# Feed-forward to attention: the first group's loads ahead of the last chunk's turn, its row products between the last query operations

## The chip, the core and the metric

The kernel runs on one core of one Trainium2 chip, as one program. The metric is the time of one execution on the device in microseconds. A core has engines that run their own instruction streams and meet only at semaphores: TensorE (PE, matrix products into the eight PSUM banks), VectorE (DVE), ScalarE (ACT), GpSimd (POOL), and the sync engine SP, which in this kernel issues every DMA, one instruction after another.

## What is computed

Four steps over x, 4 sequences of 512 tokens of 512 channels, each added to x behind a gate tanh(g):

```python
x = x + jnp.tanh(g_xattn[0]) * _L0_xattn_ref(4, 512, 512, L0_xattn_w, L0_xattn_u, _layernorm(x), ctx_2048)
x = x + jnp.tanh(g_ffn[0]) * _L0_ffn_ref(_layernorm(x), L0_ffn_w1, L0_ffn_w2, L0_ffn_w3)
x = x + jnp.tanh(g_xattn[1]) * _L1_xattn_ref(_layernorm(x), ctx_2048, wq, bq, wkv, bkv, wp, bp)
x = x + jnp.tanh(g_ffn[1]) * _L1_ffn_ref(_layernorm(x), gamma, W)
```

The change lies between the second and the third. The second is a feed-forward of 2048 hidden channels with activations rounded to 8 bits in groups of 64: silu(q(x) W1) * q(x) W2, rounded again, times W3. The third is attention with 16 heads of 32 channels:

```python
q = _qdq(x) @ _qdq(wq).T + bq            # _qdq: 8-bit rounding of each token's row
kv = cond @ wkv.T + bkv                  # keys and values, from the context
attn = softmax(einsum('bnhd,bmhd->bhnm', q, k) * scale)
o = einsum('bnhm,bmhd->bnhd', attn, v)
out = _qdq(o) @ _qdq(wp).T + bp
```

## The kernel before

**Tiles.** The 2048 tokens are 16 token tiles of 128 (TOK), four (TB) to each of 4 sequences (BATCH). The 512 channels are four blocks of 128 (DB), and each block holds one group of four heads (HG), so attention runs over 4 x 4 = 16 groups (b, g). The hidden channels are four chunks of 512 (FC). Numbers in brackets below are (token tile, chunk) or (sequence, group).

**Feed-forward.** For each token tile i and chunk j, TensorE multiplies by W1 and W2 (`up`, L1028 to L1040, line of the products L1038), ScalarE and VectorE apply silu, product and rounding, ScalarE and GpSimd write the result as a high and a low half (`high` L749, `lo_part` L532), SP turns it with a transposing DMA (`turn_h`, L389 to L394), and TensorE multiplies by W3 (`down`, L1042 to L1049) into bank 5 for even and bank 6 for odd token tiles, which VectorE adds to X (`residual`, L1475). `down(i, j)` waits for the turn `hT_in[j]`. The order of work on each engine is the order in which the program writes it; semaphores only make an engine wait.

**Queries, interleaved with it.** For token tile u: `q_stats` (DVE, L1483), `q_rstd` (POOL, L539), `q_norm` (ACT, L754), `q_max` (DVE, L1490), `q_diag` (POOL, L546), `q_round` (ACT, L760), `q_ints` (DVE, L1498), `q_turn` (PE, L1051, transposes L1056 and a diagonal product L1058), `q_operands` (ACT, L764), `q_project` (PE, L1060), `q_full` (DVE, L1503), `q_bias` (ACT, L771), `q_low` (POOL, L551). Each feeds the next. They follow the feed-forward by two to four token tiles, so the last of them stand in a tail written out by hand on every engine, behind the loop: L1086 to L1096 on TensorE, L1550 to L1564 on VectorE, L818 to L829 on ScalarE, L585 to L593 on GpSimd.

**Attention.** For a group (b, g) SP brings keys (`load_kv`, three DMAs L411 and one of values L414) and queries (`load_q`, twelve DMAs L423) into KS and QS, 16 in all. KS and QS lie in the memory of W1 and W2, so the first loads wait until the last `up` is done (`b_ps`, L404). For stability of the softmax the kernel first finds the maximum of each query's scores: 16 row products for a group (`rows`, L1101, products L1108, into banks 0, 1 and 5 in turn; each waits until the maximum of the third last has been read), and VectorE reduces each (`maxima`, L1568, L1574). TensorE turns the 16 columns of maxima (`c_turn`, L1111, L1116), ScalarE and VectorE write them as a high and a low half (`c_out` L835, `c_low` L1577), and SP sends them as two more rows of QS (`send_c`, L427, DMAs L432). GpSimd has set the matching rows 96 and 97 of KS to 1 (L597). Only then can the 16 score products of the group run (`scores`, L1119, L1125; the first waits for `c_in`), with the maxima already inside, followed by exponentials on ScalarE (L866), the products with V (`weigh`, L1135) and the sums (L1144, L1154, additions on GpSimd L610). Each group is 16 slots; the row products of the next groups are dealt out over the slots (`ROWS`, L300, with a lead of `LEAD` = 6 rows), so that the first row product of group g + 2 stands in slot 8 of group g, and `c_turn` of group g + 1 behind slot 9.

**Order on SP at the boundary.** All hidden turns up to `turn_h(15, 3)`; the wait for `b_ps`; loads of groups 0, 1, 2, 3 of sequence 0; `send_c(0, 0)` (L434 to L437); then `feed` (L439), whose first act is `send_c(0, 1)`.

**Order on TensorE at the boundary.** `down(15, 3)`, the last query operations, a wait for `area_free` (the last read of ffs by the tail of VectorE; L1099), waits that the banks are free (L1202 to L1204), 16 + 6 row products, the wait for the ones, `c_turn(0, 0)`, and the groups.

Of the kernel before, what the change touches and what calls it, by code (L numbers as in the profile page):

```python
# [8 lines left out]
ALU = mybir.AluOpType  # L9
# [7 lines left out]
DB = D // P  # L17
# [14 lines left out]
def up_to(eng, sem, value):  # L32

    if isinstance(value, int) and value <= 0:
        return
    eng.wait_ge(sem, value)


class Chain:
# [5 lines left out]
    def link(self, ins):  # L45

        ins.then_inc(self.sem, 1)
        self.n += 1
        self.eng.wait_ge(self.sem, self.base + self.n)
# [11 lines left out]
def flamingo_kernel(nc, x, ctx_2048, g_xattn, g_ffn, w, u, w1, w2, w3, wq, bq, wkv, bkv, wp, bp, gamma, wl, out):  # L61
    stack = ExitStack()
    with stack:
# [255 lines left out]
        def _(sp):  # L319
# [62 lines left out]
            def turn_x(i, a):  # L382

                sp.wait_ge(xhi, i + 1)
                sp.wait_ge(xlo, i + 1)
                up_to(sp, b_ps, FC * (i - 1))
                sp.dma_start_transpose(XQT[a], PHL.rearrange("p h d -> p (h d)")).then_inc(xT_in[a], 16)

            def turn_h(i, j):  # L389

                sp.wait_ge(hi_done, FC * i + j + 1)
                sp.wait_ge(lo_done, FC * i + j + 1)
                up_to(sp, down_ps, FC * i + j - 3)
                sp.dma_start_transpose(HT[j], HLb[j].rearrange("p h d -> p (h d)")).then_inc(hT_in[j], 16)  # L394

            sp.wait_ge(ff_scales, 1)
            turn_x(0, 0)
            for i in range(TOK):
                for j in range(FC):
                    turn_h(i, j)  # L400
                    if j == 0 and i < TOK - 1:
                        turn_x(i + 1, (i + 1) % 2)

            sp.wait_ge(b_ps, FC * TOK)  # L404

            def load_kv(b, g, first):

                if not first:
# [18 lines left out]
            def send_c(b, g):  # L427

                sp.wait_ge(ct_ready, b * DB + g + 1)
                sp.wait_ge(ct_low, b * DB + g + 1)  # L430
                for h in range(2):
                    sp.dma_start(QS[96 + h:97 + h, HG * g:HG * g + HG, :], CT[h][0:HG, :]).then_inc(c_in, 16)  # L432

            for g in range(DB):  # L434
                load_kv(0, g, True)
                load_q(0, g)
            send_c(0, 0)  # L437

            def feed(b, first, last):  # L439
                for g in range(DB):  # L440
# [19 lines left out]
        def _(pool):  # L460
# [85 lines left out]
            def q_diag(u):  # L546
                pool.wait_ge(qs3, u + 1)
                up_to(pool, sx_ps, u)
                nc.gpsimd.tensor_tensor(DIAG, id32[:, :], QSC[:, 0:1].to_broadcast([P, P]), ALU.mult).then_inc(diag3, 1)

            def q_low(u):  # L551
                pool.wait_ge(q_hi, u + 1)
                nc.gpsimd.tensor_tensor(held[:, 0:1], held[:, 1:2], held[:, 1:2], ALU.add)
                cols = bass.ds(u * P, P)
                nc.gpsimd.tensor_tensor(QALL[:, 1, :, cols], QB, QALL[:, 0, :, cols], ALU.subtract).then_inc(q_lo, 1)
# [5 lines left out]
            def tiles(k, last):  # L561
                for a in range(2):
                    i = 2 * k + a
                    for j in range(FC):
                        if j == 0 and there(i - 3):
                            q_diag(i - 3)
                        if j == 1 and not (last and a == 1):
                            x_turned(pool, k, a)
                            prep_lo(i + 1)
                        if j == 1 and not last:  # L570
                            prep(i + 2)
                        if j == 2 and there(i - 2):
                            q_rstd(i - 2)
                        if j == 2 and there(i - 4):
                            q_low(i - 4)
                        lo_part(i, j)
# [5 lines left out]
                tiles(k, False)  # L582
            step.turns_over(TOK // 2 - 3)
            tiles(TOK // 2 - 1, True)
            q_diag(TOK - 3)  # L585
            q_rstd(TOK - 2)
            q_low(TOK - 4)
            q_diag(TOK - 2)
            q_rstd(TOK - 1)
            q_low(TOK - 3)  # L590
            q_diag(TOK - 1)
            q_low(TOK - 2)
            q_low(TOK - 1)  # L593


            pool.wait_ge(q_lo, TOK)
            nc.gpsimd.memset(KS[96:98, :, :], 1.0).then_inc(ks_ones, 1)  # L597
            pool.wait_ge(ks_ones, 1)

            def add_weights(b, first, last):  # L600
                for g in range(DB):
# [33 lines left out]
        def _(act):  # L635
# [124 lines left out]
            def q_round(u):  # L760
                act.wait_ge(qs3, u + 1)
                nc.scalar.activation(LX, LX, ACT.Copy, bias=RND, scale=QR[:, 0:1]).then_inc(rnd3, 1)
# [58 lines left out]
            q_operands(TOK - 3)  # L821
            q_round(TOK - 2)
            q_norm(TOK - 1)
            q_bias(TOK - 3)
            q_operands(TOK - 2)
            q_round(TOK - 1)
            q_bias(TOK - 2)
            q_operands(TOK - 1)
            q_bias(TOK - 1)  # L829


# [94 lines left out]
        def _(pe):  # L926
# [156 lines left out]
            with pe.Fori(2, TOK // 2 - 1) as k:  # L1083
                tiles(k, False, False)
            tiles(TOK // 2 - 1, False, True)
            q_project(TOK - 4)  # L1086
            down(TOK - 1, 0, 1)
            down(TOK - 1, 1, 1)
            q_turn(TOK - 3)
            down(TOK - 1, 2, 1)  # L1090
            down(TOK - 1, 3, 1)
            q_project(TOK - 3)
            q_turn(TOK - 2)
            q_project(TOK - 2)
            q_turn(TOK - 1)
            q_project(TOK - 1)  # L1096


            pe.wait_ge(area_free, 1)  # L1099

            def rows(b, g, n):  # L1101

                j, t, r = n // TB, n % TB, (b * DB + g) * 16 + n
# [15 lines left out]
            def scores(b, g, t, j):  # L1119

                n = b * DB + g
                if t == 0 and j == 0:
                    pe.wait_ge(c_in, n * 32 + 32)
                up_to(pe, exp_done, n * 16 + HG * t + j - 1)
                mm(bank[2 + j % 2][:, :], KS[0:98, HG * g + j, t * P:t * P + P], QS[0:98, HG * g + j, :],  # L1125
                   start=True, stop=True).then_inc(st_ps, 1)
# [51 lines left out]
            def attend(b, first, last):  # L1178
                for g in range(DB):
                    opening, closing = first and g == 0, last and g == DB - 1  # L1180
                    ahead = coming(b, g)
                    for slot in range(16):
# [16 lines left out]
                        if slot == 9 and not closing:  # L1199
                            c_turn(*following(b, g))  # L1200

            pe.wait_ge(down_read, TOK)  # L1202
            pe.wait_ge(h_done, FC * TOK)
            pe.wait_ge(qf_ready, TOK)  # L1204
            for n in range(16):
                rows(0, 0, n)
            for n in range(LEAD):
                rows(0, 1, n)
            pe.wait_ge(ks_ones, 1)
            c_turn(0, 0)  # L1210
            for b in range(BATCH):
                attend(b, b == 0, b == BATCH - 1)
            weigh(BATCH - 1, DB - 1, TB - 1)
# [45 lines left out]
        def _(dve):  # L1259
# [292 lines left out]
            q_ints(TOK - 3)  # L1552
            q_full(TOK - 4)
            q_max(TOK - 2)
            residual(TOK - 1, 1)
            q_stats(TOK - 1)
            q_full(TOK - 3)
            q_ints(TOK - 2)
            link(ts(LSC, LSC, 1.0 / 127.0, None, ALU.mult))
            ts(LSC, LSC, TG[:, 3:4], None, ALU.mult).then_inc(area_free, 1)  # L1560
            q_max(TOK - 1)
            q_full(TOK - 2)
            q_ints(TOK - 1)
            q_full(TOK - 1)  # L1564

            flat = lambda a: a.rearrange("p a d -> p (a d)")

            def maxima(b, g, n):  # L1568
# [46 lines left out]
                        i = (b - 1) * TB + g  # L1615
                        reduce(OM[:, bass.ds(i, 1)], OALL[:, bass.ds(i, 1), :], AX.X, ALU.max, apply_absolute_value=True)

            for n in range(16):
                maxima(0, 0, n)
            for n in range(LEAD):  # L1620
                maxima(0, 1, n)
            c_low(0, 0)
            for b in range(BATCH):
                attend(b, b == 0, b == BATCH - 1)
            def scales(n, m):
# [106 lines left out]
```

## Time and profile before

| | |
|---|---|
| Median of 3 runs | 993.82 us (992.88 to 997.99) |
| Profiled execution | 988.19 us, its span 986.4 us |
| Mean granted TensorE clock in it | 0.931 of full speed |
| Busy in the span: PE, DVE, ACT, POOL | 83%, 78%, 59%, 49% |
| Feed-forward, last hidden turn issued | about 576 us into the span |
| First score product of attention | about 618 us into the span |

The profile's page gives for each engine its busy time, the costliest lines with their mean duration, and the chain of work that ended last: from the last instruction back, at each step to what released it. The timeline lists an engine's instructions in order of time as start, duration, engine, line, operation, operands and count; in brackets stands how long the engine was idle before it and what released it. An entry with a count merges neighbours, so its duration over its count is a pace. SPq is SP issuing DMAs: the duration is that of the issue, not of the transfer. The windows give busy time per engine in a stretch and the granted clock of TensorE, where 1.00 is 2.4 GHz and 0.50 is 1.2 GHz.

### The profile page before, as it was taken

To read this page: it belongs to the slowest core of one execution; us is meant where nothing else is said; L and a number is where in the kernel's file an instruction comes from. 1 tells how busy PE (TensorE), PEld (TensorE's weight loads), DVE (VectorE), ACT (ScalarE), POOL (GpSimd) and SP (SyncE) were. 2 spreads that over 40 slices of the span, in tenths; PEclk is the share of its full clock that TensorE was granted. 3 is DMA by queue.
4 is the path that set the end of the run, shared out by engine and by line. 5 is a ranking of instruction groups with operands and counts; after the bars stand their busy time and mean duration, and the time that the engine had idled before them with its cause. 6 is when DMAs were issued, how large, how long until landed. Compare 5 with 4: busy or idle time off the path is not lost.

```text
span 986.4 us, 15339 instructions
## 1 busy us (share of the span) xinstructions
PE 816.1 (83%) x4423; PEld 356.8 (36%) x4423; DVE 766.1 (78%) x1499; ACT 579.3 (59%) x1025; POOL 483.7 (49%) x556
## 2 busy tenths in 40 slices
PE   1279989818999999999999966899999999865654
PEld 1245445403444444454444431222222222222221
DVE  3969999866899989999999756677777777635885
ACT  2368988733445556565666452566666666656662
POOL 1186564212344444343443333575757575746561
PEclk9589999969999999999999985899999999997886
DMA  8548996622233332323233233112121211000111
GB/s 281 210 118 213 236 215 184 185 66 45 57 62 71 58 64 53 64 53 64 53 61 67 54 95 97 37 52 77 54 77 54 75 55 44 2 1 0 47 59 64
DMA packets 165162, 84.49 MB, mean 86 GB/s; under 512 B 116961, under 2 KB 149873, under 8 KB 165105
## 3 DMA queue, kind: packets, MB, share of 16 engines
q1 hardware_dynamic: 165104, 83.81, 33.7%
q8 instruction: 26, 0.43, 0.2%
q14 instruction: 32, 0.25, 0.1%
HBM read 37.50 MB, written 12.58 MB: 51 GB/s over the span
## 4 chain that ended last, share of the span: by engine, by line
PE 54%; DVE 9%; issue 4%; SPq 4%; ACT 4%; DMA 3%; POOL 1%; DVEq 0%; ACTq 0%; POOLq 0%
PE bank L1038 21%; PE bank L1047 10%; PE bank L1135 5%; PE bank L1108 5%; PE bank L1125 4%; SPq L423 3%; DMA A<-B 3%; PE bank L1144 2%; PE bank L1154 2%; PE bank L1065 1%; DVE X L1683 1%; SPq L432 1%; DVE B L1582 1%; DVE B L1668 1%; ACT B L839 1%
## 5 line engine op out<-in xcount | busy, mean ns | idle before, releaser
L1038 PE MATMUL bank<-A,B 128*128 128x512 f16 x1024 | 232.9, 381 | 18.6 <-DMA B<-B 14.8
L1574 DVE TENSOR_REDUCE B<-bank 128x1 f32<-128x512 f32 x256 | 167.6, 683 | 68.6 <-PE bank L1108 68.5
L866 ACT ACTIVATE A<-bank 128x512 f32<-128x512 f32 x256 | 143.8, 593 | 101.9 <-PE bank L1125 97.1
L537 POOL TENSOR_TENSOR B<-B 128x512 f16<-128x512 f32 x64 | 75.5, 1180 | 207.0 <-ACT B L752 153.0
L1038 PEld LDWEIGHTS bank<-A,B 128*128 128x128 f16 x1024 | 100.2, 98 | 141.5 <-issue 18.3
L610 POOL TENSOR_TENSOR B<-A 128x512 f32<-128x512 f32 x64 | 79.4, 1271 | 94.8 <-ACT A L866 94.8
L1047 PE MATMUL bank<-A,B 128*128 128x512 f16 x512 | 120.6, 379 | 0.0
L1125 PE MATMUL bank<-A 98*128 98x512 f16 x256 | 93.3, 385 | 25.4 <-DMA A<-B 13.8
L747 ACT ACTIVATE bank<-B 128x512 f32<-128x512 f32 x64 | 38.5, 602 | 124.2 <-DVE B L1467 123.9
L1108 PE MATMUL bank<-A 96*128 96x512 f16 x256 | 98.8, 408 | 1.2 <-DVE B L1506 1.1
L610 POOL TENSOR_TENSOR B<-B,A 128x512 f32<-128x512 f32 x64 | 79.1, 1267 | 0.0
L1047 PEld LDWEIGHTS bank<-A,B 128*128 128x128 f16 x512 | 49.5, 98 | 54.2 <-DMA B<-B 0.3
L1135 PE MATMUL bank<-A,B 128*32 128x512 f32 x512 | 68.2, 605 | 1.0 <-ACT A L866 1.0
L1462 DVE SCALAR_TENSOR_TENSOR bank<-bank,ffs,B 128x512 f32<-128x512 f32 x64 | 48.3, 755 | 14.6 <-PE bank L1038 11.4
L1473 DVE SCALAR_TENSOR_TENSOR B<-bank,B 128x512 f32<-128x512 f32 x64 | 44.2, 691 | 17.1 <-ACT bank L747 15.7
L1016 PE MATMUL bank<-B 128*128 128x512 f16 x192 | 44.2, 380 | 12.4 <-DVE B L1368 12.4
L1108 PEld LDWEIGHTS bank<-A 96*128 96x128 f16 x256 | 23.0, 99 | 79.8 <-DVE B L1574 69.7
L1125 PEld LDWEIGHTS bank<-A 98*128 98x128 f16 x256 | 24.8, 98 | 72.0 <-ACT A L866 37.6
L499 POOL TENSOR_SCALAR B<-X,mv,rs 128x128 f32<-128x128 f32 x64 | 49.9, 795 | 1.2 <-DVE WLT L1296 1.2
L742 ACT ACTIVATE B<-bank,ffs 128x512 f32<-128x512 f32 x64 | 43.0, 671 | 9.5 <-PE bank L1038 9.3
L752 ACT CAST B<-B 128x512 f16<-128x512 f32 x64 | 39.5, 618 | 11.3 <-DVE B L1473 10.9
L1464 DVE TENSOR_REDUCE B<-bank 128x8 f32<-128x512 f32 x64 | 44.3, 691 | 2.2
(232 smaller groups left out, 1495.3 us busy)
## 6 DMA issues: line engine op xcount, KB each, us to landing
B<-in_L_ffn_w_dram SPq DMA_DIRECT2D x48, 256.0 KB, 3.2
A<-k_parts SPq DMA_DIRECT2D x48, 128.0 KB, 2.5
A<-B SPq DMA_DIRECT2D x192, 32.0 KB, 1.9
X<-in_x_dram SPq DMA_DIRECT2D x4, 1024.0 KB, 13.6
B<-in_ctx_dram SPq DMA_DIRECT2D x16, 256.0 KB, 5.2
k_parts<-B SPq DMA_DIRECT2D x16, 256.0 KB, 4.6
v_rows<-B SPq DMA_DIRECT2D x16, 256.0 KB, 3.0
B<-v_rows SPq DMA_DIRECT2D x16, 256.0 KB, 3.2
```

The source lines that it names most:

```text
L499: last_ = nc.gpsimd.tensor_scalar(XN[:, t, cols], X[:, i, cols], mv[:, i:i + 1, 0], rs[:, i:i + 1], ALU.subtract, ALU.mult)
L537: nc.gpsimd.tensor_tensor(HLb[j][:, 1, :], Db[j % 2], HLb[j][:, 0, :], ALU.subtract).then_inc(lo_done, 1)
L610: nc.gpsimd.tensor_tensor(ACC[j], PR[j] if t == 1 else ACC[j], PR[(HG * t + j) % 8], ALU.add).then_inc(acc_done, 1)
L866: nc.scalar.activation(PR[(HG * t + j) % 8], bank[2 + j % 2][:, :], ACT.Exp, scale=SCALE).then_inc(exp_done, 1)
L1038: last = mm(bank[2 * n + q][:, :], XQT[a][:, m, :], wt[:, m % DB, j * 512:j * 512 + 512], start=(m == 0), stop=(m == 2 * DB - 1))
L1047: last = mm(bank[5 + q][:, :], HT[j][:, m, :], W3T[:, DB * j + m % DB, :], start=(j == 0 and m == 0), stop=(j == FC - 1 and m == 2 * DB - 1))
L1108: mm(bank[ROW_BANKS[r % 3]][:, :], QS[0:96, HG * g + j, t * P:t * P + P], KS[0:96, HG * g + j, :], start=True, stop=True).then_inc(row_ps, 1)
L1125: mm(bank[2 + j % 2][:, :], KS[0:98, HG * g + j, t * P:t * P + P], QS[0:98, HG * g + j, :], start=True, stop=True).then_inc(st_ps, 1)
L1135: last_ = mm(bank[6][DH * j:DH * j + DH, :], VB[:, t, (HG * g + j) * DH:(HG * g + j + 1) * DH], PR[(HG * t + j) % 8], start=(t == 0), stop ...
L1462: stt(H, H, C2, SAb[q], ALU.mult, ALU.mult).then_inc(h_done, 1)
L1464: link(reduce(gsm[:, 0, :], grouped(H), AX.X, ALU.max, apply_absolute_value=True))
L1574: reduce(NMX[g % 2][:, t, j:j + 1], bank[ROW_BANKS[r % 3]][:, :], AX.X, ALU.max, negate=True).then_inc(row_max, 1)
```

## The change

On SP the loads of group 0 stand before the last hidden turn, behind the wait for `b_ps`; the loads of group 1 behind that turn; then `send_c(0, 0)`; then the loads of groups 2 and 3. On TensorE and VectorE the 16 row products and maxima of group (0, 0) are dealt out in the tail: two ahead of `down(15, 3)` and `residual(15)`, six between the last query operations, eight behind the last projection. TensorE no longer waits for `area_free`, but waits for the banks that the rows take (`d_done`, `down_read` of tile 14) ahead of the first. `c_turn(0, 0)` stands ahead of the six row products of group (0, 1), and on VectorE `c_low(0, 0)` behind the first of their maxima. On ScalarE `q_bias(13)` and `q_bias(14)` stand one place later, on VectorE `q_ints(14)` stands ahead of `q_full(13)`. On GpSimd the one memset of the ones becomes four, one for each group of heads, put between the last `q_low`; TensorE's wait for them moves into `scores`.

```diff
@@ SP @@
+            sp.wait_ge(ff_scales, 1)
+            turn_x(0, 0)
+            for i in range(TOK):
+                for j in range(FC):
+                    if i == TOK - 1 and j == FC - 1:
+                        sp.wait_ge(b_ps, FC * TOK)
+                        load_kv(0, 0, True)
+                        load_q(0, 0)
+                    turn_h(i, j)
+                    if j == 0 and i < TOK - 1:
+                        turn_x(i + 1, (i + 1) % 2)
+            load_kv(0, 1, True)
+            load_q(0, 1)
+            send_c(0, 0)
+            for g in range(2, DB):
                 load_kv(0, g, True)
                 load_q(0, g)
-            send_c(0, 0)
@@ GpSimd @@
+            def ones_under(g):
+
+                pool.wait_ge(b_ps, FC * TOK)
+                pool.wait_ge(diag3, TOK)
+                if g > 0:
+                    pool.wait_ge(q_lo, TOK - DB + 1 + g)
+                nc.gpsimd.memset(KS[96:98, HG * g:HG * g + HG, :], 1.0).then_inc(ks_ones, 1)
+                pool.wait_ge(ks_ones, g + 1)
...
-            q_low(TOK - 3)
             q_diag(TOK - 1)
-            q_low(TOK - 2)
-            q_low(TOK - 1)
-
-
-            pool.wait_ge(q_lo, TOK)
-            nc.gpsimd.memset(KS[96:98, :, :], 1.0).then_inc(ks_ones, 1)
-            pool.wait_ge(ks_ones, 1)
+            ones_under(0)
+            for u in (TOK - 3, TOK - 2, TOK - 1):
+                q_low(u)
+                ones_under(u - TOK + 4)
@@ ScalarE @@
             q_norm(TOK - 1)
-            q_bias(TOK - 3)
             q_operands(TOK - 2)
             q_round(TOK - 1)
+            q_bias(TOK - 3)
+            q_operands(TOK - 1)
             q_bias(TOK - 2)
-            q_operands(TOK - 1)
             q_bias(TOK - 1)
@@ TensorE: the tail of before is taken out, and scores has @@
                     pe.wait_ge(c_in, n * 32 + 32)
+                    if b == 0:
+                        pe.wait_ge(ks_ones, g + 1)
@@ TensorE @@
+            q_project(TOK - 4)
+            down(TOK - 1, 0, 1)
+            down(TOK - 1, 1, 1)
+            q_turn(TOK - 3)
+            down(TOK - 1, 2, 1)
+            pe.wait_ge(d_done, FC * TOK)
+            pe.wait_ge(down_read, TOK - 1)
+            first_rows(0, 2)
+            down(TOK - 1, 3, 1)
+            q_project(TOK - 3)
+            first_rows(2, 3)
+            q_turn(TOK - 2)
+            first_rows(3, 4)
+            q_project(TOK - 2)
+            first_rows(4, 6)
+            q_turn(TOK - 1)
+            first_rows(6, 8)
+            q_project(TOK - 1)
+            first_rows(8, 16)
             pe.wait_ge(down_read, TOK)
             pe.wait_ge(h_done, FC * TOK)
             pe.wait_ge(qf_ready, TOK)
-            for n in range(16):
-                rows(0, 0, n)
+            c_turn(0, 0)
             for n in range(LEAD):
                 rows(0, 1, n)
-            pe.wait_ge(ks_ones, 1)
-            c_turn(0, 0)
@@ VectorE @@
+            first_maxima(0, 2)
+            residual(TOK - 1, 1)
+            q_stats(TOK - 1)
+            q_ints(TOK - 2)
+            q_full(TOK - 3)
+            link(ts(LSC, LSC, 1.0 / 127.0, None, ALU.mult))
+            ts(LSC, LSC, TG[:, 3:4], None, ALU.mult).then_inc(area_free, 1)
+            first_maxima(2, 3)
+            q_max(TOK - 1)
+            first_maxima(3, 4)
+            q_full(TOK - 2)
+            q_ints(TOK - 1)
+            first_maxima(4, 8)
+            q_full(TOK - 1)
+            first_maxima(8, 16)
+            maxima(0, 1, 0)
+            c_low(0, 0)
+            for n in range(1, LEAD):
                 maxima(0, 1, n)
-            c_low(0, 0)
```

## Rows read from the trace of the kernel before

**Rows 1.** The page, section 4: the chain that ended last, by line.

```profile
PE bank L1038 21%; PE bank L1047 10%; PE bank L1135 5%; PE bank L1108 5%; PE bank L1125 4%; SPq L423 3%; DMA A<-B 3%; PE bank L1144 2%; PE bank L1154 2%; PE bank L1065 1%; DVE X L1683 1%; SPq L432 1%; DVE B L1582 1%; DVE B L1668 1%; ACT B L839 1%
```

**Rows 2.** The same chain in order of time, 560 to 640 us: start, us, what.

```profile
615.80 0.69 SPq L432
...
618.29 0.61 PE bank L1125
```

**Rows 3.** Timeline of SP, two windows: start, us, engine, line, operation, count.

```profile
569.96 6.48 SPq L394 DMA_TRANSPOSE B<-B  x2
...
575.21 1.23 SPq L394 DMA_TRANSPOSE B<-B  x1
...
576.49 1.53 SPq L411 DMA_DIRECT2D A<-k_parts  x3
...
586.95 1.53 SPq L411 DMA_DIRECT2D A<-k_parts  x3
...
606.14 1.53 SPq L411 DMA_DIRECT2D A<-k_parts  x3
```

**Rows 4.** DMA issues of the whole kernel: operands, count, KB each, us to landing.

```profile
A<-B SPq DMA_DIRECT2D x192, 32.0 KB, 1.9
...
B<-B SPq DMA_TRANSPOSE x80, 3.1
```

**Rows 5.** Timeline of TensorE, 576 to 626 us, in the columns of rows 3.

```profile
576.68 3.62 PE L1047 MATMUL bank<-A,B 128*128 128x512 f16 x16
580.45 1.07 PE L1065 MATMUL bank<-B,WQT 128*128 128x128 f16 x16 [0.15 <-ACT B L769]
...
591.11 0.74 PE L1058 MATMUL bank<-B,ones 128*128 128x128 f32 x2
593.36 1.89 PE L1065 MATMUL bank<-B,WQT 128*128 128x128 f16 x16 [1.51 <-ACT B L769]
596.33 12.74 PE L1108 MATMUL bank<-A 96*128 96x512 f16 x22 [1.09 <-DVE B L1506]
608.87 1.06 PE L1116 MATMUL bank<-id,B 128*4 128x128 f32 x4
...
625.12 0.38 PE L1108 MATMUL bank<-A 96*128 96x512 f16 x1
```

**Rows 6.** Timeline of VectorE, 580 to 612 us.

```profile
580.78 0.73 DVE L1481 SCALAR_TENSOR_TENSOR X<-bank,ffs,X 128x512 f32<-128x512 f32 x1
...
584.84 0.69 DVE L1494 TENSOR_REDUCE B<-B 128x1 f32<-128x512 f32 x1 [1.14 <-ACT B L758]
...
595.28 0.69 DVE L1506 TENSOR_TENSOR B<-bank,B 128x512 f32<-128x512 f32 x1 [4.63 <-PE bank L1065]
596.96 13.25 DVE L1574 TENSOR_REDUCE B<-bank 128x1 f32<-128x512 f32 x22 [0.99 <-PE bank L1108]
610.91 0.68 DVE L1582 TENSOR_TENSOR B<-bank,B 4x512 f16<-4x512 f32 x1 [0.71 <-ACT B L839]
```

**Rows 7.** Windows, attention's groups 0 and 1: stretch, us, busy by engine, clock, DMA.

```profile
618.29:632.83 14.54, 13.41 (x61) 3.86 (x62) 10.58 (x17) 9.00 (x17) 9.34 (x8) 0.87 0.01 2
632.83:649.26 16.43, 15.37 (x93) 4.63 (x94) 11.90 (x20) 10.29 (x20) 11.55 (x10) 1.00 0.23 64
```

**Rows 8.** Windows of 2 us: where the granted clock fell and came back.

```profile
584.00:586.00 2.00, 0.12 (x2) 0.00 (x0) 1.00 (x3) 2.00 (x5) 0.00 (x0) 0.62 0.18 49
...
608.00:610.00 2.00, 2.00 (x7) 0.69 (x6) 2.00 (x4) 0.00 (x0) 0.00 (x0) 0.50 0.80 236
...
622.00:624.00 2.00, 1.96 (x13) 0.45 (x11) 1.98 (x4) 1.68 (x3) 0.51 (x1) 1.00 0.00 0
```

**Rows 9.** Timeline of ScalarE, 592 to 600 us.

```profile
592.55 0.58 ACT L768 COPY B<-bank 128x512 f16<-128x512 f16 x1
...
598.32 1.28 ACT L832 ACT_TABLE_LOAD   x1
```

**Rows 10.** Timeline of GpSimd, the memset of the ones.

```profile
599.73 6.92 POOL L597 MEMSET A<- 2x8192 f16 x1
```

More of the change, by code:

```diff
@@ L394, in turn_h @@
                 sp.dma_start_transpose(HT[j], HLb[j].rearrange("p h d -> p (h d)")).then_inc(hT_in[j], 16)
[L396 to L404, printed above, removed]
             def load_kv(b, g, first):
@@ L432, in send_c @@
                     sp.dma_start(QS[96 + h:97 + h, HG * g:HG * g + HG, :], CT[h][0:HG, :]).then_inc(c_in, 16)
-            for g in range(DB):
+            sp.wait_ge(ff_scales, 1)
[13 more added lines that the diff above has]
+            for g in range(2, DB):
                 load_kv(0, g, True)
                 load_q(0, g)
-            send_c(0, 0)
             def feed(b, first, last):
@@ L1085, in _ @@
             tiles(TOK // 2 - 1, False, True)
[L1086 to L1099, printed above, removed]
             def rows(b, g, n):
@@ L1200, in attend, with first_rows @@
                             c_turn(*following(b, g))
+            def first_rows(n, m):
+                for r in range(n, m):
+                    rows(0, 0, r)
+            q_project(TOK - 4)
[17 more added lines that the diff above has]
+            first_rows(8, 16)
             pe.wait_ge(down_read, TOK)
@@ L1554, in _ @@
             q_max(TOK - 2)
[L1555 to L1564, printed above, removed]
             flat = lambda a: a.rearrange("p a d -> p (a d)")
@@ L1616, in attend, with first_maxima @@
                         reduce(OM[:, bass.ds(i, 1)], OALL[:, bass.ds(i, 1), :], AX.X, ALU.max, apply_absolute_value=True)
-            for n in range(16):
-                maxima(0, 0, n)
-            for n in range(LEAD):
+            def first_maxima(n, m):
+                for r in range(n, m):
+                    maxima(0, 0, r)
+            first_maxima(0, 2)
[16 more added lines that the diff above has]
+            for n in range(1, LEAD):
                 maxima(0, 1, n)
-            c_low(0, 0)
             for b in range(BATCH):
```

## The prediction

> **What bounds the kernel now.** I read the chain that ended last first. TensorE leads it over the whole span, but one line of the sync queue, L423, holds 3% of it, about 29 us [rows 1]. The same chain in order of time shows where it ends: the sync engine (SP) issues the small transfer of L432 at 615.80, and the first score product (L1125) starts at 618.29 [rows 2]; the 36 us ahead of 615.80 are the issuing of loads. So at this boundary the issuing of DMAs is the bound, not any engine that computes. The timeline of SP gives the pieces: the turn of the last hidden chunk, turn_h(15,3), is issued at 575.21, then four groups of 16 loads each. The second, third and fourth start 9.6 us apart (586.95, 596.55, 606.14), the first took 10.5, and send_c(0,0) is issued behind the fourth at 615.80 [rows 2, 3]. Next the computing engines: TensorE's query operations end at 595.3, its 22 row products run from 596.33 to 609, paced by VectorE's maxima (22 in 13.25 us, 0.60 each), and the row of maxima is ready to send at 611.6, 4.2 us before SP is free [rows 5, 6]. Hence the loads delay the first score by only 4.2 us; without them the chain of the maxima would be next.
>
> **What has to be costed is the second send, not the first.** In both versions send_c(0,1) stands on SP behind the loads of groups 2 and 3. Before, these were long past: group 0 of attention took 14.54 us, and group 1's first score ran at 632.83. From there a group takes 16.43 us [rows 7]. After the change the loads of groups 2 and 3 (2 x 9.6 us) stand between send_c(0,0) and send_c(0,1). If send_c(0,0) is issued at T, then the second send is issued at T + 1.36 (two issues and their gaps) + 19.2 = T + 20.6, and group 1's first score starts 2.5 us behind its issue, as 615.80 and 618.29 stood, at T + 23.1 [rows 2, 3]. What follows is the same work at the same 16.43 us, so the change is worth 632.83 - (T + 23.1): break-even is **T = 609.7**.
>
> **T, step by step.**
> Load of group 0: SP issues turn_h(15,2) from 569.96 for 1.23 us; the weights' last use is past by 569.1, so the load starts at 571.2 and ends at 580.8 (9.6; with the first group's 10.5 it would be 581.7). Its last issue lands 1.9 us after it starts, at 582.1 [rows 3, 4].
> Turn of the last chunk: issued at 575.21 before, 580.9 now. It lands about 3.1 us behind its issue [rows 4], at 584.0. What is queued behind it is down(15,3), 5.7 us later than before. Two row products stand ahead of it on TensorE and wait for the load, 578.4 to 582.1, but they are done before 584.0 and cost nothing of their own.
> Clock: the granted clock fell to its lower level (1.2 GHz) at about 584.5, 3 us after the dense work ended at 581.5; here dense work ends at 578.4 and 3.7 idle us follow. I take the lower level, 0.50 in the rows [rows 5, 8]. Then down(15,3), 8 products, takes 3.4 us instead of 1.7 (sixteen took 3.62 at the upper level; a projection took 1.07 there and 1.89 at the lower [rows 5]) and ends at 587.4.
> Query chain of token tile 15: its residual starts at 587.5. From residual to q_max took 4.06 us (580.78 to 584.84) through statistics, GpSimd and ScalarE, unchanged by the new order, so q_max(15) starts at 591.6 [rows 6]. ScalarE's q_norm(15) is done then, q_operands(14) follows (0.8, from 592.55 to TensorE's 593.36 [rows 5, 9]), TensorE's q_project(14) runs 592.4 to 594.3, and q_full(14) and q_ints(15), 0.7 and 0.4, end at 595.4. q_turn(15) takes 1.1 (591.11 + 0.74, begun at 590.7) to 596.6, q_operands(15) goes to 597.5, q_project(15) and q_full(15) take 1.92 + 0.69 as before: 600.1 [rows 5, 6]. Before, q_full(15) ended at 595.97, so the query chain ends **4.1 us later**, although it started 5.7 to 6.7 later: ScalarE's reordering takes q_bias(13) out from between.
> Maxima: eight of sixteen are dealt into gaps of this chain, eight are left: 8 x 0.60 = 4.8, to 604.9, where 13.25 stood before. The dealt ones lie in waits of VectorE (4.6 us stood before q_full(15) alone [rows 6]).
> Maxima row: c_turn's start to the end of c_low took 2.7 us (608.87 to 611.59 [rows 5, 6]); now one maximum stands between, hidden by ScalarE's copy except 0.2. So **T = 608**.
> The other edits: q_bias(15) follows q_full(15) and q_low(14) and ends on ScalarE at about 603.5, with the 1.28 us table load [rows 9] 604.8, ahead of the copy at 606.5. The memset (6.92 us for all heads [rows 10]) becomes four; I take a quarter each, 1.7 us, with 0 to 1 us more per piece as bounds, since no smaller one is in the trace; group 0's is over by 596 and GpSimd's q_low is off the path until 604.9. The new SP wait on send_c(0,0) blocks the loads of groups 2 and 3 while SP is idle from 591.8 to 608: this is the price of the change, and it is in the 23.1.
>
> **The sum.** Group 1's first score at 608 + 23.1 = 631.1: 1.7 us earlier. On the way TensorE waits twice. Slot 8 of group 0 needs group 2's load, T + 12.3, and would be reached at T + 2.5 + 6.8 (618.29 to 625.12 before [rows 2, 5]): 3.0 us idle. And at group 1's first score it waits from about T + 19.2 to T + 23.1: 3.9 us. The clock fell after such a gap at 584.5, and in attention it came back at 622, 3.7 us behind the first score [rows 2, 8]; 3.7 us at half rate cost 1.9, if every product is on the path. Some are not: TensorE has about 1 idle us per group (15.37 busy of 16.43 [rows 7]). I take 1.2, bounds 0 and 2.4. Net gain 0.5 us: the profiled run's 988.2 becomes 987.7. The median of the shown runs is 993.8, 5.6 above; on that scale **993.3**.
>
> The page "DMA: Bandwidth & Descriptors" of the Trainium skill (Queues, rings and completion order) says that a transfer's completion is written only after all earlier writes of that DMA engine. This speaks against putting 16 loads ahead of the turn. The loads' 1.9 us to landing, against the turn's 3.1, would put them down first, so by the rule and by the rows the turn lands at 584.0 alike; were the loads slower to drain, T would grow by that.
>
> **Rivals.**
> *Clock stays up, short chain (0.12).* If TensorE's five dense microseconds after 584 bring the clock back, or it never falls, down(15,3) takes 1.7, each projection 1.07, and ScalarE's queue becomes the limit: q_project(15) ends at 595.9 and T is 604.1. Group 1 starts at 627.2, 5.6 us earlier: 988.2, or about 990 with the clock lost in the waits. For it: dense work was followed by the upper level at 622. Against: 12.7 us of row products paced by VectorE were not [rows 5, 8]. Most of this case is a gain of 2 to 5 us, within 0.5%.
> *The held-back chunk costs more than is won (0.20).* Mechanism: turn_h(15,3) and all of tile 15's query chain behind the load. It decides from T = 609.7, that is with 1.7 us more than I sum: 0.9 if the first load again takes 10.5, and any microsecond that rows between the query operations take from ScalarE's or VectorE's waits. With T = 610.6 and both waits costing the clock (2.4), group 1's work is 3.3 us late: 997.1.
> *SP's second and third loads do not bind (0.05).* If the whole 7.7 us by which the first score comes earlier (T + 2.5 = 610.5 against 618.29) reached the end: 986.1. Against it stands only the order on SP, 38 issues with none faster than 0.43 us, and I see no way round it.
> *The change does nothing at all (in the forecast).* SP's order makes the end of the boundary T + 23.1, and T moves by less than 2 us: that is close to what I forecast.
>
> **How the numbers follow.** Forecast 0.63 for a net of -1.4 to +2.6 us; rivals 0.12, 0.20, 0.05. A measurement of this kernel tells 0.5%, 5 us, from no change. Faster by more: the third rival and a third of the first, 0.09. Slower by more needs T above 612: 0.05. Range: 987.5 (short chain, 988.2) to 998.0 (the slow rival, 997.1), each rounded outwards because the runs shown lay 992.9 to 998.0.
>
> **What would show it.** Right: SP's last turn near 581, a gap on SP before send_c(0,0) at about 608, two waits of TensorE on loads at slot 8 and on L432 in front of group 1, group 1's first score near 631, 16.4 us per group after. Wrong: send_c(0,0) before 604 or after 611; granted clock at the upper level from 588 to 605; group 1's first score more than 3 us from 631; or a group of attention that is no longer 16.4 us.

## The result: 0.3% slower

The changed kernel takes 997.8 us (median of 19 runs, 995.5 to 1000.7), the kernel before 994.9 in 19 runs of the same sessions (991.8 to 998.3). The ratio is **1.0031, 95% interval 1.002 to 1.0043**: about 3 us more. The time lies in the stated range, but the sign was forecast the other way (0.5 us less).

| | before | after |
|---|---|---|
| Median of 19 runs | 994.91 us | 997.82 us |
| Span of the profiled execution | 986.4 us | 994.8 us |
| Mean granted clock | 0.931 | 0.934 |

The two spans are 8.4 us apart, which is more than the change costs. To see only what the change touches, I measure a **boundary** inside each trace: from the start of q_ints(13) on VectorE (t0; the last work on VectorE that is the same in both) to the first score product of group (0,2), from where each group takes 16.43 us again. Before, that is 575.70 to 649.26 us: 73.56. After, 580.67 to 657.97: 77.30, so **3.74 us more**. The 5.0 us by which t0 itself differs belong to unchanged work; in the nine traces below t0 lies between 575.55 and 583.18.

The kernel before, t0 and the first score product of groups 1 and 2:

```profile
575.70 0.41 DVE L1501 TENSOR_SCALAR B<-B 128x512 f16<-128x512 f32 x1
...
632.83 0.38 PE L1125 MATMUL bank<-A 98*128 98x512 f16 x1 [0.41 <-ACT A L866]
...
649.26 0.38 PE L1125 MATMUL bank<-A 98*128 98x512 f16 x1 [0.41 <-DMA A<-B]
```

The changed kernel, t0:

```profile
580.67 0.41 DVE L1516 TENSOR_SCALAR B<-B 128x512 f16<-128x512 f32 x1
```

A boundary is read from one profiled execution, a ratio from all runs of a version. For every version below the two give the same sign, and sizes within 2 us of each other, so tenths of a microsecond in a boundary are exact readings of one trace and not averages.

The timeline of SP in the changed kernel, in the columns of rows 3 (L394 the turns, L401 keys, L413 queries, L422 the row of maxima):

```profile
574.92 1.23 SPq L394 DMA_TRANSPOSE B<-B  x1
576.21 1.53 SPq L401 DMA_DIRECT2D A<-k_parts  x3
...
586.07 1.28 SPq L394 DMA_TRANSPOSE B<-B  x1
587.39 1.54 SPq L401 DMA_DIRECT2D A<-k_parts  x3
...
615.54 1.35 SPq L422 DMA_DIRECT2D A<-B  x2
616.93 1.38 SPq L401 DMA_DIRECT2D A<-k_parts  x3
...
628.48 8.29 SPq L413 DMA_DIRECT2D A<-B  x12
636.87 1.32 SPq L422 DMA_DIRECT2D A<-B  x2
```

send_c(0,0) goes out 34.87 us behind t0 instead of 40.10 [rows 2]: 5.2 us earlier. Then the two groups of loads fill SP from 616.93 to 636.8, and only behind them send_c(0,1) is issued, 21.3 us after the first. TensorE in the same stretch (L1120 scores, L1101 row products):

```profile
618.04 0.61 PE L1120 MATMUL bank<-A 98*128 98x512 f16 x1
...
627.77 0.38 PE L1101 MATMUL bank<-A 96*128 96x512 f16 x1 [2.04 <-issue]
...
639.37 0.61 PE L1120 MATMUL bank<-A 98*128 98x512 f16 x1 [4.55 <-DMA A<-B]
...
657.97 0.38 PE L1120 MATMUL bank<-A 98*128 98x512 f16 x1 [0.41 <-DMA A<-B]
```

The first score runs 37.4 us behind t0, where it had run at 42.6. TensorE then stands 2.0 us at slot 8 (marked as issue; the last query load of group 2 was issued at 625.80 and lands about 1.9 us later) and 4.55 us in front of group 1, and group 1's first score comes at 58.7 where it came at 57.1. All 5.2 us of the earlier send are gone, and 1.6 more. The rest of the loss lies in group 1, and it is the clock; windows as in rows 7 and 8:

```profile
637.00:638.00 1.00, 0.00 (x0) 0.00 (x0) 0.00 (x0) 0.00 (x0) 0.00 (x0) 0.64 0.13 35
...
643.00:644.00 1.00, 1.00 (x3) 0.15 (x1) 0.72 (x2) 0.00 (x0) 0.00 (x0) 0.50 0.16 27
644.00:645.00 1.00, 1.00 (x9) 0.17 (x8) 0.56 (x1) 0.60 (x1) 0.00 (x0) 0.95 0.96 279
...
639.37:657.97 18.60, 17.54 (x92) 4.85 (x93) 11.57 (x19) 10.06 (x19) 9.79 (x8) 0.87 0.21 57
657.97:674.40 16.43, 15.37 (x92) 4.61 (x92) 11.90 (x20) 10.30 (x20) 11.10 (x10) 1.00 0.23 66
```

In the wait the granted clock fell to 1.2 GHz and was back at 2.4 GHz only at 644; group 1 took 18.60 us instead of the 16.43 of rows 7, with the same products. All of it lies in the first products: from the group's first score to its first sum (L1149; L1154 in the kernel before) it took 4.65 us where it had taken 2.49, and eight products with V took 1.93 us instead of 1.06. Together 1.57 + 2.17 = 3.74 us.

### The profile page after: what moved, and what is told of

The parts are those of the page before. It is cut to its first block, busy times and chain, and to the rows that moved or that the text cites. A ratio compares the mean times of both kernels' runs of the same rounds, so it can differ in the third digit from the quotient of the medians.

```text
span 994.8 us, 15350 instructions
## 1 busy us (share of the span) xinstructions
PE 821.2 (83%) x4423; PEld 359.6 (36%) x4423; DVE 767.2 (77%) x1499; ACT 579.9 (58%) x1025; POOL 485.2 (49%) x559
## 4 chain that ended last, share of the span: by engine, by line
PE 53%; DVE 9%; issue 5%; SPq 4%; ACT 4%; DMA 3%; POOL 1%; DVEq 0%; ACTq 0%; POOLq 0%
PE bank L1046 21%; PE bank L1055 10%; PE bank L1130 5%; PE bank L1101 4%; PE bank L1120 4%; DMA A<-B 2%; SPq L413 2%; PE bank L1139 2%; PE bank L1149 2%; PE bank L1073 1%; SPq L422 1%; DVE X L1705 1%; DVE B L1586 1%; DVE B L1690 1%; PE bank L1109 1%
## 5 line engine op out<-in xcount | busy, mean ns | idle before, releaser
L1046 PE MATMUL bank<-A,B 128*128 128x512 f16 x1024 | 233.0, 381 | 18.6 <-DMA B<-B 14.8
L1120 PE MATMUL bank<-A 98*128 98x512 f16 x256 | 94.5, 390 | 21.4 <-ACT A L874 10.9
L1101 PE MATMUL bank<-A 96*128 96x512 f16 x256 | 97.1, 405 | 8.1 <-DMA A<-B 3.8
L1101 PEld LDWEIGHTS bank<-A 96*128 96x128 f16 x256 | 23.1, 100 | 83.2 <-DVE B L1578 66.1
L1120 PEld LDWEIGHTS bank<-A 98*128 98x128 f16 x256 | 25.0, 99 | 67.3 <-ACT A L874 36.5
```

What stands on the lines that cost most here:

```text
L1046: last = mm(bank[2 * n + q][:, :], XQT[a][:, m, :], wt[:, m % DB, j * 512:j * 512 + 512], start=(m == 0), stop=(m == 2 * DB - 1))
L1101: mm(bank[ROW_BANKS[r % 3]][:, :], QS[0:96, HG * g + j, t * P:t * P + P], KS[0:96, HG * g + j, :], start=True, stop=True).then_inc(row_ps, 1)
```

## The experiments

Two theories. **A**: the two loads between the sends on SP cost the time; everything hangs on T, the issue of send_c(0,0), and on what stands behind it. **B**: the held-back turn and the dealt-out rows cost it, whatever the order of the loads. Each run's numbers are counted from its own t0. "S1" is the first score of group 1.

| kernel | send_c(0,0) | send_c(0,1) | S1 | boundary | ratio to before |
|---|---|---|---|---|---|
| before | 40.10 | 54.60 | 57.13 | 73.56 | 1 |
| changed | 34.87 | 56.20 | 58.70 | 77.30 | 1.0031 [1.002, 1.0043] |
| a_load2_first | 34.92 | 50.36 | 52.88 | 69.32 | 0.9953 [0.994, 0.9966] |
| b_send_early | 35.96 | 57.16 | 59.66 | 77.69 | 1.0047 [1.0032, 1.0063] |
| b_load3_late | 35.98 | 50.96 | 53.49 | 69.92 | 0.9953 [0.9939, 0.9966] |
| a_second_qf | 32.32 | 53.71 | 56.21 | 74.86 | 1.0019 [1.0008, 1.0031] |
| b_hold_load3_late | 43.19 | 58.10 | 60.63 | 77.06 | 1.0026 [1.0013, 1.0038] |
| b_cturn_first | 33.80 | 49.36 | 51.88 | 68.31 | 0.9928 [0.9903, 0.9953] |
| v_turn_first | 29.13 | 43.99 | 46.51 | 62.94 | 0.989 [0.9874, 0.9906] |

**1. The changed kernel, only one group of loads behind the send.**

```diff
-            load_kv(0, 1, True)
-            load_q(0, 1)
-            send_c(0, 0)
-            for g in range(2, DB):
+            for g in range(1, DB - 1):
                 load_kv(0, g, True)
                 load_q(0, g)
+            send_c(0, 0)
+            load_kv(0, DB - 1, True)
+            load_q(0, DB - 1)
```

> The changed kernel, with the loads of group 2 put ahead of send_c(0,0), and only those of group 3 behind it. I measure the boundary from the start of q_ints(13) on VectorE (the same work before it in all kernels) to the first score product of group 2: 73.56 us before the change, 77.30 after. Theory A, sends behind loads: send_c(0,1) stood behind two loads, now behind one, which is done before the second row of maxima is ready. send_c(0,0) stays at 34.9 us, group 1's first score comes 17.0 us behind it (2.5 to the first score, 14.5 for group 0) instead of 23.8, with no wait of TensorE for a load at slot 8 and no fall of the clock: boundary 68.3 us, 5.2 below before and 9.0 below the change, ratio to before 0.995. Theory B, the held-back last turn and the dealt-out rows cost the time: the order of these loads changes nothing, boundary 77, ratio 1.003.

Measured: the first send where it was (34.92), the second 5.8 us earlier, boundary 69.32, ratio 0.9953. Sixteen DMA instructions, moved ahead of the two of one send, turn a loss of 0.3% into a gain of 0.5%. Its TensorE has no wait at slot 8, and in front of group 1's first score one of 0.41 us, as the kernel before had:

```profile
629.09 0.39 PE L1120 MATMUL bank<-A 98*128 98x512 f16 x1 [0.32 <-ACT A L874]
...
632.79 0.38 PE L1120 MATMUL bank<-A 98*128 98x512 f16 x1 [0.41 <-DMA A<-B]
```

Theory B would have left the boundary at 77. The miss of 1.0 us against my 68.3 lies between the first score and S1, 15.5 us instead of 14.5. The granted clock came back only between 623 and 624 there (0.76 in that window), about 6 us behind the first score at 617.33, where it had been 3.7 before.

**2. The kernel before, with nothing but the early send.**

```diff
-            for g in range(DB):
+            for g in range(2):
                 load_kv(0, g, True)
                 load_q(0, g)
             send_c(0, 0)
+            for g in range(2, DB):
+                load_kv(0, g, True)
+                load_q(0, g)
```

> The kernel before, with nothing of the change but the place of send_c(0,0): behind the loads of groups 0 and 1, ahead of those of groups 2 and 3. Theory A: the row of maxima is ready 35.9 us into the boundary and is sent then, 4.2 earlier than before, but send_c(0,1) stands behind two loads: group 1's first score 23.8 us behind it at 59.7, before 57.13, and with the clock lost in the wait (2.2, as in the changed kernel) a boundary of 78.4 us, 4.8 above before; ratio 1.005. Theory B: nothing of the query chain is touched, the send is earlier, so the boundary is 4 us shorter, 69.4, ratio 0.996.

Measured: 77.69 and 1.0047, against 78.4 and 1.005 expected. No query operation is touched, no turn held, no row dealt out; the early send alone makes the kernel slower, by sending the first row 4.1 us earlier. TensorE shows the same two waits:

```profile
627.87 0.38 PE L1111 MATMUL bank<-A 96*128 96x512 f16 x1 [2.44 <-issue]
...
639.34 0.39 PE L1128 MATMUL bank<-A 98*128 98x512 f16 x1 [4.43 <-DMA A<-B]
...
657.37 0.38 PE L1128 MATMUL bank<-A 98*128 98x512 f16 x1 [0.41 <-DMA A<-B]
```

From 639.34 to 657.37 is 18.03 us for group 1, again over 16.43. The windows have the clock at 1.00 through the wait and at 0.50 from 640 to 643: here it fell only when the products had begun again. That is a second measurement of what such a wait costs through the clock, 1.6 us.

**3. The kernel before, one group of loads behind the send.** As run 2, with `range(3)` and `range(3, DB)`.

> The kernel before, with only the loads of group 3 moved behind send_c(0,0). Theory A: send_c(0,0) when its row is ready, at 35.9 us of the boundary; group 3's loads are over 11 us later, before the second row is ready at about 14.4; group 1's first score 17.0 us behind the send; boundary 69.4 us, 4.2 below before, ratio 0.996. Theory B gives the same for this one; a boundary of 73.6 would say that the loads in front of the send were not what the first score waited for.

Measured: 69.92, ratio 0.9953.

```profile
618.15 1.34 SPq L432 DMA_DIRECT2D A<-B  x2
...
633.13 1.32 SPq L432 DMA_DIRECT2D A<-B  x2
```

Moving one group of loads is a gain, moving two is a loss. And this simplest edit, one group of loads moved on one engine, has the same ratio as run 1, which carries all of the change's reordering: holding, dealing out, moving c_turn and the new order on ScalarE together bring the first send from 35.98 to 34.92, 1.06 us.

**4. What made T later than I summed.** The changed kernel with a second buffer for the scaled query of tile 14. q_full(14) then waits for no q_bias, and q_full(15) for q_bias(13) and no longer for q_bias(14). (q_bias is changed to read QF2 for tile 14; not shown.)

```diff
+        QF2 = part(D, F32, "p (k t) -> p k t", k=DB)
+        fourteen = lambda u: isinstance(u, int) and u == TOK - 2
...
             def q_full(u):
                 dve.wait_ge(qp_ps, u + 1)
-                up_to(dve, q_hi, u)
-                tt(QF, bank[7][:, :].rearrange("p (k t) -> p k t", k=DB),
+                if not fourteen(u):
+                    up_to(dve, q_hi, u - 1 if isinstance(u, int) and u == TOK - 1 else u)
+                tt(QF2 if fourteen(u) else QF, bank[7][:, :].rearrange("p (k t) -> p k t", k=DB),
```

> The changed kernel with a second buffer for the scaled query of token tile 14, so that q_full(14) no longer waits for q_bias(13), which the change had put behind q_norm(15) and q_round(15) on ScalarE. Theory A2, this wait is the largest part of what the send of the first row came later than I summed: q_full(14) starts when q_project(14) is done and VectorE is free, 2.4 us earlier than in the changed kernel; send_c(0,0) 2.3 us earlier (32.6 us into the boundary against 34.9), and as everything hangs on this send, the boundary 75.0 against 77.30; ratio to before 1.001. Rival: ScalarE's queue or the slower q_ints is next at once, and send_c(0,0) moves by less than 1 us.

Measured: send_c(0,0) at 32.32, 2.55 us earlier, boundary 74.86. The changed kernel around the wait that is gone here: TensorE's q_project(14) (L1073), the last step of q_bias(13) on ScalarE (L787), and VectorE (L1521 q_full, L1516 q_ints):

```profile
597.73 1.07 PE L1073 MATMUL bank<-B,WQT 128*128 128x128 f16 x16 [1.81 <-ACT B L777]
...
600.47 0.62 ACT L787 CAST B<-B 128x512 f16<-128x512 f32 x1
...
601.19 0.69 DVE L1521 TENSOR_TENSOR B<-bank,B 128x512 f32<-128x512 f32 x1 [2.46 <-ACT B L787]
601.80 1.01 DVE L1516 TENSOR_SCALAR B<-B 128x512 f16<-128x512 f32 x1
```

and with the second buffer:

```profile
602.10 0.69 DVE L1524 TENSOR_TENSOR B<-bank,B 128x512 f32<-128x512 f32 x1 [0.93 <-PE bank L1075]
602.70 0.56 DVE L1518 TENSOR_SCALAR B<-B 128x512 f16<-128x512 f32 x1
```

q_full(14) starts 18.92 us behind t0 instead of 20.52, released by the projection and not by ScalarE. Of the 2.55 us, 1.60 are this wait. Another 0.46 come from q_ints(15), which took 0.56 us and not 1.01, and the remaining 0.49 lie in front of q_full(15), which in the changed kernel was released by q_bias(14) on ScalarE and here by its projection. Run 1 shows from the other side that the projection did not bind in the changed kernel: its q_project(14) took 1.89 us, 0.8 more, and q_full(14) started at 20.58 all the same. Everything behind moved with the send, as theory A has it.

**5. The price of the held-back turn alone.** Run 3, and the 16 loads of group 0 ahead of `turn_h(15, 3)` as in the change. The diff is against run 3 and shows only the held turn.

```diff
                 for j in range(FC):
+                    if i == TOK - 1 and j == FC - 1:
+                        sp.wait_ge(b_ps, FC * TOK)
+                        load_kv(0, 0, True)
+                        load_q(0, 0)
                     turn_h(i, j)
```

> The kernel before with only the loads of group 3 behind send_c(0,0), as in the run with that change alone (boundary 69.92 us, send at 35.98), and now also the 16 loads of group 0 ahead of the last hidden turn. It costs what the hold costs by itself, without dealt-out rows to pay for it. My sum: the turn 5.9 us later, down(15,3) at the lower clock, residual(15) at 12.3 us of the boundary instead of 5.1, the query chain behind it 7.2 to 7.7 later, send_c(0,0) at 43.6 us, boundary 77.6, ratio to before 1.004. The rival, that the hold is cheap because other query work fills the wait: send_c(0,0) by 38 us, boundary 72, ratio 0.998.

Measured: residual(15) at 12.28 us instead of 5.08, send_c(0,0) 7.21 us later than in run 3, boundary 77.06 (7.1 more). In the timeline of VectorE the whole tail has slid, with the wait for down(15,3) in front and the 22 maxima behind as in rows 6:

```profile
593.64 0.75 DVE L1486 SCALAR_TENSOR_TENSOR X<-bank,ffs,X 128x512 f32<-128x512 f32 x1 [7.12 <-PE bank L1052]
...
609.84 13.24 DVE L1579 TENSOR_REDUCE B<-bank 128x1 f32<-128x512 f32 x22 [0.98 <-PE bank L1113]
```

So the hold is not cheap: it costs 7.2 us of the chain, and what run 1 adds to it, dealt-out rows, the earlier c_turn and the new order on ScalarE, returns 8.3 (43.19 to 34.92). Theory B is right about the price and wrong about the verdict: the price is paid back, and 1.1 us more.

**6. The earlier c_turn alone.** Run 3, and c_turn(0,0) ahead of the six rows of group (0,1) on TensorE, c_low(0,0) behind the first of their maxima on VectorE. The diff shows TensorE's part against run 3.

```diff
+            c_turn(0, 0)
             for n in range(LEAD):
                 rows(0, 1, n)
             pe.wait_ge(ks_ones, 1)
-            c_turn(0, 0)
```

> The kernel before with the loads of group 3 behind send_c(0,0), and c_turn(0,0) and c_low(0,0) put ahead of the row products and maxima of group (0,1), as the change does. With the send no longer waiting for loads, the chain of the maxima sets it: six maxima of 0.60 us less in front, one of them kept ahead of c_low at a cost of 0.2: send_c(0,0) at 32.5 us of the boundary instead of 35.98, boundary 66.4 against 69.92, ratio to before 0.993. The rival, that the first scores then wait for those six rows anyway: boundary above 69.

Measured: 33.80, boundary 68.31, ratio 0.9928. Of the 3.5 us that I expected 2.2 came. c_turn now has to wait for the last maximum, where before six rows had stood between, and starts 2.2 us earlier instead of 3.6:

```profile
611.73 1.01 PE L1119 MATMUL bank<-id,B 128*4 128x128 f32 x4 [1.18 <-DVE B L1577]
```

Without holding or dealing anything its boundary is 1.0 us shorter than that of run 1, and its first send 1.1 us earlier. The two ratios point the same way, but their intervals overlap. By the traces, then, holding, dealing out and the new order on ScalarE together are a small loss in run 1. They need not be: run 4 takes 2.55 us off the same chain by removing the waits for q_bias. Run 1 with the second buffer was not measured.

**7. A version that beats both.** Keys and values of group 0 ahead of the turn, its query loads behind; loads of group 2 ahead of the send; rows dealt out where VectorE waits in the trace of before; ScalarE's order as before; the memsets behind the last q_low. TensorE has four rows behind q_turn(14), two behind q_project(14), three behind q_turn(15) and seven behind q_project(15).

```diff
                     if i == TOK - 1 and j == FC - 1:
                         sp.wait_ge(b_ps, FC * TOK)
                         load_kv(0, 0, True)
-                        load_q(0, 0)
                     turn_h(i, j)
...
+            load_q(0, 0)
@@ VectorE @@
             q_max(TOK - 1)
+            first_maxima(0, 4)
             q_full(TOK - 2)
             q_ints(TOK - 1)
+            first_maxima(4, 9)
             q_full(TOK - 1)
+            first_maxima(9, 16)
```

> The changed kernel with four repairs: the last hidden turn goes out before the query loads of group 0 (only its three key loads and one value load stand ahead of the turn, in 4 us in which SP waits anyway); the loads of group 2 ahead of send_c(0,0); the rows of group (0,0) dealt out where VectorE waits in the trace of before (four between q_max(15) and q_full(14), five between q_ints(15) and q_full(15), seven at the end) with ScalarE's order as before; the four memsets behind the last q_low. My sum: the query chain as before, q_full(15) at 19.6 us of the boundary, seven maxima and the turn of the maxima after it, send_c(0,0) at 27.5 us, when the loads of group 2 are just out; group 1's first score 17.5 later, boundary 61.5 against 73.56 before and 77.30 in the changed kernel, ratio to before 0.988. If the dealt-out rows delay the query operations (TensorE or VectorE taken when a query operation is due), q_full(15) comes later than 20.5 and the boundary lies near 65.

Measured: boundary 62.94, **ratio 0.989 (0.9874 to 0.9906)**, 983.8 us. VectorE's maxima now lie in its waits:

```profile
586.10 2.48 DVE L1577 TENSOR_REDUCE B<-bank 128x1 f32<-128x512 f32 x4 [0.35 <-PE bank L1102]
...
591.94 1.89 DVE L1577 TENSOR_REDUCE B<-bank 128x1 f32<-128x512 f32 x3 [0.26 <-PE bank L1102]
594.30 0.69 DVE L1520 TENSOR_TENSOR B<-bank,B 128x512 f32<-128x512 f32 x1 [0.47 <-PE bank L1074]
594.91 4.26 DVE L1577 TENSOR_REDUCE B<-bank 128x1 f32<-128x512 f32 x7
```

q_full(15) starts at 18.75 us, even before the 19.58 of the kernel before, since the last projection ran at the upper clock (1.07 us, 1.89 in rows 5):

```profile
593.19 1.07 PE L1074 MATMUL bank<-B,WQT 128*128 128x128 f16 x16 [0.86 <-ACT B L778]
```

The granted clock was 0.50 from 585 to 591, 0.72 from 591 to 592 and 1.00 after that. Before it rose, TensorE had run rows, projection and turn from 585.48 on with no wait above 0.27 us; in the kernel before, with no rows between, it waited 3.58, 1.12 and 1.51 us between the same operations, and the clock stayed at 0.50. The row of maxima is ready at 26.5, but SP is still issuing the loads of group 2, and the send goes out at 29.13, 1.6 us behind my 27.5, which is the whole of the 1.4 us by which the boundary missed. SP is the bound again; what would move it further, fewer or cheaper issues, was not tried. The profiled execution is the fastest of the six (977.13 us; the others 982.75 to 985.77), and this run changes four things at once: it shows what they give together, not each by itself.

## Why the prediction was wrong

**Right: what bounds, and the formula.** The chain behind T was S1 = T + 23.1. Measured, T + 23.8 in the changed kernel: 0.7 too little, because the two groups of loads took 19.9 us and not 19.2 (one query load was issued in 1.33 us instead of 0.59). Run 2 gives T + 23.7. The two waits of TensorE were forecast with 3.0 and 3.9 us, they were 2.0 and 4.55. Break-even T was put at 34.0 behind t0; T came at 34.87. (The "38 issues" of the third rival are 36: 32 loads and two for each send. Nothing hangs on it.)

**Wrong: the sum for T, 32.3 behind t0, measured 34.87.** Point by point, from t0:

| step | summed | measured |
|---|---|---|
| turn of the last chunk issued | 5.2 | 5.40 |
| residual(15) starts | 11.8 | 12.28 |
| q_max(15) starts | 15.9 | 16.40 |
| q_project(14) ends | 18.6 | 18.13 |
| q_full(14) starts | 18.6 | 20.52 |
| q_ints(15) done | 19.7 | 22.14 |
| c_turn(0,0) can start | 29.2 | 32.04 |
| send_c(0,0) | 32.3 | 34.87 |

The hold itself, its 5.7 us on SP, the lower clock in down(15,3) and the 4.06 us from residual to q_max were right within 0.5. The step that failed is "q_project(14) runs 592.4 to 594.3, and q_full(14) and q_ints(15) end at 595.4". I let q_full(14) start when the projection was done. But q_full also waits for q_hi, that is for q_bias of the tile before, because the scaled query has one buffer, and the change moved q_bias(13) behind q_norm(15) and q_round(15) on ScalarE. The prediction called this reordering a help ("takes q_bias(13) out from between") and costed q_bias(15) with care, but never asked who waits for q_bias(13). The prediction's own numbers imply it: q_max(15) from 591.6, 1.1 us to its end, 0.7 for q_round(15) and 2.3 for q_bias(13) give 595.7, not 594.3. So 1.4 of the 2.57 us by which T was late are this wait, and the prediction could have had them: they put T at 609.4, next to its break-even. Another 0.5 had gathered by q_max(15), and 0.5 is q_ints(15), which took 1.01 us. Run 4 shows that the wait is real: with the buffer doubled T falls by 2.55 us, to 32.32. That this is my sum to 0.02 is in part luck, since the run also lost the slow q_ints(15) and the wait in front of q_full(15), while its q_full(14) came 0.3 later than summed. Even so the boundary is then 74.86, 1.3 above before, so the sign would still have been wrong.

One thing went better than summed and gave nothing. I took the lower clock for q_project(14); in the changed kernel's trace the granted clock was back at 1.00 from 593 to 599, behind down(15,3) and the work next to it, and fell to 0.50 again by 600. The projection took 1.07 us and ended half a microsecond early, but q_full(14) was waiting for ScalarE. The fast rival, in which the clock comes back, was thus half true; that ScalarE's queue then becomes the limit it had right as well, but it put T at 604.1, and on that scale T was 610.6.

**Wrong: the clock's price.** I took 1.2 us of bounds 0 to 2.4; it was 2.2 (18.60 against 16.43), in run 2 1.6, in run 4 2.2 (56.21 to 74.86 is 18.65). The idle microsecond per group did not absorb it. This is the term that turns the sign once T is right: in run 4 S1 comes 0.9 us earlier than before (56.21 against 57.13), and group 1 then takes 2.2 more. My own bound of 2.4 would have given a loss of 0.7 even with my T.

Together: 2.6 of T, 0.7 of the loads and 1.0 of the clock are 4.3 us, which lead from my gain of 0.5 to the measured 3.74. The slow rival came out closest: it put T at 610.6, and 610.57 was measured on that scale, and its loss at 3.3 us. That it hit so well is luck. It named a slower first load (10.5 us; measured 9.7) and rows that take time from ScalarE or VectorE; neither happened, and the hold cost what I had summed. Of its two waits only the second cost the clock: behind the wait at slot 8 each product took 0.38 us as before. But its form, that anything more in the chain turns the gain into a loss, was right, and it held 0.20, too little for a margin of 1.7 us that rested on a chain of a dozen steps, in which a wait that is overlooked makes T later and never earlier.

## What to carry to other kernels

An in-order DMA queue has to be costed for the second and third transfer behind a moved one, not only for the one that is pulled forward: here one group of loads moved behind the send won 0.5% and two lost 0.5% (runs 3 and 2). For every operation that is put later, look for who waits for it through a shared buffer, in the helper's own waits and not only in the order of the streams. And a wait of a few microseconds on TensorE in front of a dense stage is to be priced with the slower clock behind it, 1.6 to 2.2 us here.

## What the runs showed of the hardware beyond that

A VectorE instruction took 1.01 us instead of 0.41 in the changed kernel: q_ints(15) at 601.80, while GpSimd ran q_low(13) (the first line below). In the kernel before it took 0.42, with no GpSimd instruction beside it.

```profile
601.38 1.15 POOL L558 TENSOR_TENSOR B<-B 128x512 f16<-128x512 f32 x1
602.68 1.88 POOL L594 MEMSET A<- 2x2048 f16 x1
```

In run 4 it took 0.56, from 602.70, and there a memset of GpSimd was still running:

```profile
601.18 1.80 POOL L596 MEMSET A<- 2x2048 f16 x1
```

It ended 0.28 us behind GpSimd's instruction both times (602.81 and 602.53; 603.26 and 602.98). The Trainium skill, page "SBUF — State Buffer", section "SBUF: two separate sides", says that the two engines share a port pair which one of them holds for a whole instruction while the other waits, for VectorE instructions of certain kinds. Both times agree with it. No run here took GpSimd's instruction away alone, though, and q_ints(14) of the kernel before took only 0.42 us (582.97) beside a small GpSimd operation of 128x1 (582.81 to 583.42), so the cause is argued and not shown. The memset of a quarter took 1.80 to 1.88 us, a quarter of the 6.92 of rows 10 within 0.15.

The turn that was issued behind 16 loads landed in 3.20 us, against 3.1 in rows 4: the transfers ahead of it cost it at most 0.1 us, their issuing 5.9. The loads had landed by 587.35, when the first row product started, 1.9 us before the turn did.
